# Adding three biases on TensorE instead of GpSimd in a stack of retention, experts and attention

## The reference, cut to what matters

```python
# x is (4, 512, 128): 4 sequences of 512 tokens, 128 channels
x = x + stack(layernorm(x))          # two layers of retention and feed-forward, below
x = x + experts(layernorm(x))        # the 2 best of 8 experts per token
x = x + attention(layernorm(x))      # causal, 16 heads of 8
x = x + experts(layernorm(x))

def stack(x):
    D = make_decay(512)
    for i in range(2):
        ln_x = layer_norm(x, ln1_g[i], ln1_b[i])
        q, k, v, xo = split(ln_x @ proj_w[i] + proj_b[i], 4)
        scores = einsum('bhld,bhmd->bhlm', q, k) * D
        ret = einsum('bhlm,bhmd->bhld', scores, v)        # 16 heads of 8, back to 128 channels
        ret = (ret * silu(xo)) @ reto_w[i] + reto_b[i]
        x = x + ret
        h = layer_norm(x, ln2_g[i], ln2_b[i])
        x = x + gelu(h @ ffn1_w[i] + ffn1_b[i]) @ ffn2_w[i] + ffn2_b[i]
    return layer_norm(x, lnf_g, lnf_b)

def attention(x):
    ...                                                   # q, k, v, causal softmax
    return out @ Wo.T + bo
```

## Time and profile before

| | |
|---|---|
| time, median of three runs (lowest to highest) | 947.39 us (946.0 to 948.69) |
| the profiled execution's own time | 948.85 us |
| its span in the profile | 947.0 us |
| mean granted clock of TensorE, share of full speed | 0.856 |
| instructions | 19447 |

### The profile page before, as it was taken

The page is one execution under the profiler, slowest core; times in us unless marked ns, Lnnn a source line. Parts: engine busy times, 40 slices in busy tenths (PEclk is TensorE's granted clock), DMA queues, the critical chain, the costliest instruction groups (busy, mean ns, idle before and its releaser), DMA issues. The chain is left out here.

```text
span 947.0 us, 19447 instructions
## 1 busy us (share of the span) xinstructions
PE 654.9 (69%) x6492; PEld 449.2 (47%) x6492; DVE 582.2 (61%) x1765; ACT 344.0 (36%) x597; POOL 356.8 (38%) x674
## 2 busy tenths in 40 slices
PE   2688784587885311999914589888778972499990
PEld 0345453244554311999912134444434441398990
DVE  7978833688925580666751477667458734366663
ACT  2223242333352411444405035545444561243430
POOL 1323321124352374677746300111311323367771
PEclk9799998799997555999966579989889995699995
DMA  9201299211120011555534710420420000254544
GB/s 227 83 23 46 83 185 165 67 45 49 43 62 1 17 51 49 158 156 152 158 110 111 161 24 3 104 46 8 119 48 9 19 18 12 76 164 129 164 136 142
DMA packets 100035, 81.02 MB, mean 86 GB/s; under 512 B 7516, under 2 KB 91932, under 8 KB 99196
## 3 DMA queue, kind: packets, MB, share of 16 engines
q1 hardware_dynamic: 95152, 70.18, 30.8%
q0 software_dynamic: 4544, 9.38, 2.9%
q10 hardware_dynamic: 240, 0.20, 0.1%
HBM read 54.56 MB, written 23.20 MB: 82 GB/s over the span
## 5 line engine op out<-in xcount | busy, mean ns | idle before, releaser
L1264 DVE TENSOR_REDUCE rmax<-PA 128x1 f32<-128x512 f32 (+3 forms) x256 | 120.4, 489 | 88.0 <-PE PA L1978 81.3
L756 POOL DMA_INDIRECT outs_dram<-va,ids x78 | 96.4, 1236 | 56.7 <-DVE va L1204 30.9
L741 POOL DMA_INDIRECT rows_dram<-va,idx x64 | 63.8, 997 | 104.5 <-DVE va L1147 86.7
L1935 PE MATMUL PC<-ffn_w,pm 128*128 128x128 f32 x624 | 88.3, 285 | 11.1 <-DMA ffn_w<-in_w 10.7
L1705 PE MATMUL P<-const,xn 128*128 128x128 f32 x92 | 18.7, 340 | 98.0 <-ACT xn L1487 32.8
L1978 PE MATMUL PA<-kst,qst 96*128 96x512 bf16 (+3 forms) x256 | 84.6, 336 | 0.0
L1935 PEld LDWEIGHTS PC<-ffn_w,pm 128*128 128x128 f32 x624 | 76.3, 193 | 14.7 <-DMA ffn_w<-in_w 13.9
L1194 DVE SCALAR_TENSOR_TENSOR pm<-PB,invb,decay 128x512 f32<-128x512 f32 x78 | 58.1, 745 | 38.0 <-ACT decay L1552 36.9
L1976 PE MATMUL PA<-mqb,idb 128*128 128x128 bf16 x256 | 60.7, 238 | 28.7 <-DMA qst<-qst 14.7
L1544 ACT ACTIVATE kv_b<-P 128x256 f16<-128x256 f16 x78 | 29.9, 383 | 132.4 <-PE P L1914 132.4
L1976 PEld LDWEIGHTS PA<-mqb,idb 128*128 128x128 bf16 x256 | 25.6, 100 | 90.2 <-issue 40.8
(11 more groups left out here) (241 smaller groups left out, 1491.8 us busy)
## 6 DMA issues: line engine op xcount, KB each, us to landing
ffn_w<-in_w SPq DMA_DIRECT2D x78, 256.0 KB, 2.9
rows_dram<-wall SPq DMA_DIRECT2D x1, 8385.0 KB, 50.7
X<-in_w SPq DMA_DIRECT2D x32, 256.0 KB, 2.9
proj_w<-rows_dram SPq DMA_DIRECT2D x78, 65.0 KB
qst<-parts_dram SPq DMA_DIRECT2D x12, 384.0 KB
kst<-parts_dram SPq DMA_DIRECT2D x12, 384.0 KB
parts_dram<-qkp SPq DMA_DIRECT2D x16, 256.0 KB, 2.6
X<-in_x SPq DMA_DIRECT2D x8, 256.0 KB, 4.5
```

Source lines behind the costliest of these rows:

```text
L741: nc.gpsimd.indirect_dma_start(out=rows_dram, out_offset=bass.IndirectOffsetOnAxis(ap=idx[:, t, r:r + 1], axis=0), in_=xrow[:, t, :], in_o ...
L756: nc.gpsimd.indirect_dma_start(out=outs_dram, out_offset=bass.IndirectOffsetOnAxis(ap=ids[:, k % YB:k % YB + 1], axis=0), in_=ysb[:, k % Y ...
L1264: nc.vector.tensor_reduce(rmax[:, i, h % HG:h % HG + 1], PA[:, n % 2, 0:(i + 1) * P], AX_X, ALU.max).then_inc(pair_sb[n % 2], 1)
L1935: ins = mm(PC[:, k % 2, 0:D], eT[:, k % 2, f, :], w2b[k % WB2][:, f, :], start=f == 0, stop=f == FB - 1)
```

## The change

The 20 additions of GpSimd go, with `add_bias` and its three callers, their three semaphores and VectorE's waits for these. In their place TensorE adds each bias to the accumulator: behind the matmul (or the four matmuls) that makes a tile's 128x128 result stands one more into the same place, with `start=False`, so that it accumulates. Its weights are `one_row`, a row of 128 ones on one partition (a part of the constants that are there already), and its moving operand is the bias's own row on partition 0: the product of a column of ones and a row. That is 32 float32 matmuls in retention (a tile and layer each), 32 in feed-forward and 16 in attention, 80 in all. The last matmul of a group now carries the count to the semaphore. The loads of the biases stay as they are.

```diff
--- before.py
+++ after.py
@@ -435,9 +435,6 @@
         state_sb = sem("state_sb")
         ro_ps = sem("ro_ps")
         ro_up = sem("ro_up")
-        reto_added = sem("reto_added")
-        ffn2_added = sem("ffn2_added")
-        bo_added = sem("bo_added")
         f1_ps = sem("f1_ps")
         f1_sb = sem("f1_sb")
         f2_ps = sem("f2_ps")
@@ -680,27 +677,6 @@
                 link(nc.gpsimd.tensor_tensor(w, y, mvr[:, b % 2, :, 0], ALU.mult))
                 nc.gpsimd.tensor_scalar(w, w, -1.0, None, ALU.mult).then_inc(nrm_sb, 1)
 
-            def add_bias(acc, s, bias):
-
-                r = slice(TPS * s, TPS * s + TPS)
-                return nc.gpsimd.tensor_tensor(acc[:, r, :], acc[:, r, :], bias.unsqueeze(1).to_broadcast([P, TPS, D]),
-                                               ALU.add)
-
-            def add_reto(layer, s):
-
-                pool.wait_ge(xn_ready, BY_DVE.index(1 + 2 * layer) * SEQ + s + 1)
-                add_bias(R, s, reto_b[:, layer, :]).then_inc(reto_added, 1)
-
-            def add_ffn2(layer, s):
-
-                pool.wait_ge(xn_act, BY_ACT.index(2 + 2 * layer) * SEQ + s + 1)
-                add_bias(R, s, ffn2_b[:, layer, :]).then_inc(ffn2_added, 1)
-
-            def add_bo(s):
-
-                pool.wait_ge(xn_act, BY_ACT.index(LNC) * SEQ + s + 1)
-                add_bias(X, s, bo[:, :]).then_inc(bo_added, 1)
-
             def decay_k(g):
 
                 pool.wait_ge(kv_sb, g + 1)
@@ -763,18 +739,9 @@
                     decay_k(layer * NT + t)
                     if t == 0 and layer == 0:
                         pool.wait_ge(in_ffn, in_ffn_n)
-                        for s in range(SEQ):
-                            add_reto(layer, s)
                     if t % TPS == 2 and t > TPS:
                         norm_factors(layer * SEQ + t // TPS - 1)
-                    if t % TPS == 1 and t > 2 * TPS:
-                        add_ffn2(layer, t // TPS - 2)
                 norm_factors(layer * SEQ + SEQ - 1)
-                for s in range(SEQ - 2, SEQ):
-                    add_ffn2(layer, s)
-                if layer + 1 < LAYERS:
-                    for s in range(SEQ):
-                        add_reto(layer + 1, s)
             pool.wait_ge(in_ffn, in_ffn_n)
             pool.wait_ge(rg_sb, LAYERS * NT)
             pool.wait_ge(re_ps, LAYERS * NT)
@@ -803,8 +770,6 @@
                     norm_factors(A + 2)
                     part_rests(1)
                     norm_factors(A + 3)
-                    for s in range(SEQ):
-                        add_bo(s)
                     for s in range(SEQ - 1):
                         if s + 2 < SEQ:
                             part_rests(s + 2)
@@ -949,7 +914,6 @@
                 def add_out(t):
                     g = layer * NT + t
                     dve.wait_ge(ro_ps, g + 1)
-                    dve.wait_ge(reto_added, g // TPS + 1)
                     nc.vector.tensor_tensor(R[:, t, :], PC[:, 0, 2 * D:3 * D], R[:, t, :], ALU.add).then_inc(ro_up, 1)
 
                 def sums(t):
@@ -1000,7 +964,6 @@
                     b = layer * SEQ + s
                     r = slice(TPS * s, TPS * s + TPS)
                     dve.wait_ge(f2_ps, b + 1)
-                    dve.wait_ge(ffn2_added, b + 1)
                     nc.vector.tensor_tensor(R[:, r, :], PC[:, b % 2, :].rearrange("p (k n) -> p k n", k=TPS),
                                             R[:, r, :], ALU.add).then_inc(f2_up, 1)
                     dve.wait_ge(f2_up, b + 1)
@@ -1296,7 +1259,6 @@
                 def add_out(s):
                     n = PAIR[("wo", s)]
                     dve.wait_ge(pair_ps, n + 1)
-                    dve.wait_ge(bo_added, s + 1)
                     r = slice(TPS * s, TPS * s + TPS)
                     nc.vector.tensor_tensor(X[:, r, :], PA[:, n % 2, :].rearrange("p (i n) -> p i n", i=TPS),
                                             X[:, r, :], ALU.add).then_inc(pair_sb[n % 2], 1)
@@ -1680,6 +1642,7 @@
         @block.tensor
         def _(pe):
             mm = nc.tensor.matmul
+            one_row = const[0:1, C_ONES:C_ONES + P]
 
             def ring(*key):
 
@@ -1829,7 +1792,8 @@
                     if g >= 1:
                         pe.wait_ge(ro_up, g)
                     o = PC[:, 0, 2 * D:3 * D]
-                    mm(o, rgT[:, g % 2, :], reto_w[:, layer, :], start=True, stop=True).then_inc(ro_ps, 1)
+                    mm(o, rgT[:, g % 2, :], reto_w[:, layer, :], start=True, stop=False)
+                    mm(o, one_row, reto_b[0:1, layer, :], start=False, stop=True).then_inc(ro_ps, 1)
 
                 def ahead_turn(s):
 
@@ -1883,8 +1847,9 @@
                                 count(0, 0).then_inc(ring_ps, 1)
                         bank = PC[:, b % 2, k * D:(k + 1) * D]
                         for f in range(FB):
-                            ins = mm(bank, hT[:, b % 2, f, k * P:(k + 1) * P], ffn2_w[:, layer, f, :], start=f == 0,
-                                     stop=f == FB - 1)
+                            mm(bank, hT[:, b % 2, f, k * P:(k + 1) * P], ffn2_w[:, layer, f, :], start=f == 0,
+                               stop=False)
+                        ins = mm(bank, one_row, ffn2_b[0:1, layer, :], start=False, stop=True)
                     ins.then_inc(f2_ps, 1)
 
 
@@ -2040,7 +2005,8 @@
                     wait_pair(pe, "ao", s)
                     for i in range(TPS):
                         o = bank[:, i * D:(i + 1) * D]
-                        ins = mm(o, aoT[:, i * P:(i + 1) * P], wo, start=True, stop=True)
+                        mm(o, aoT[:, i * P:(i + 1) * P], wo, start=True, stop=False)
+                        ins = mm(o, one_row, bo[0:1, :], start=False, stop=True)
                     ins.then_inc(pair_ps, 1)
 
                 def run(uses):
```

## The result

The changed kernel takes 971.58 us (median of four runs, 970.03 to 973.22) against 946.69 us for the kernel before beside it (944.77 to 948.69): a ratio of 1.0263, 95% interval 1.0234 to 1.0291, or 24.9 us slower. Forecast were 965.7 us, 18.3 us of loss, with a range of 953 to 973. The sign, the range and the main mechanism held; about a quarter of the loss was not in the sum, and the measured time lies nearer to the rival "dearer" (973.6 us) than to the forecast. The profiled execution took 973.22 us, 24.4 more than the profiled one of before.

A forecast was written before the change was run, and what follows sets the result against it. No engine fills the span; retention is bound by TensorE and VectorE, late feed-forward and routing by a dependent chain. Exposed biases, 6.8 + 5.7 + 2.3 + 3.5 = 18.3 us, gave 965.7 us, range 953 to 973.

The forecast's parts named there:

- dearer: Retention's cover too short: another nine biases pass (5.6 us) and one covered attention projection (2.3 us): 973.6 us; chance 0.15.
- The price of a bias, 0.62 us: TensorE, each bias between two 128x128 matmuls: 0.22 us for its columns plus two changes of shape at 0.2 us.
- The choice between the ends: Per bias on TensorE: 0.62 us if one row is treated like 32 rows (taken), 0.22 if like 96.
- cheap: All added matmuls on TensorE: one row runs like 96, no change of shape, 7.3 us lost, 954.7 us; chance 0.18.
- GpSimd worth nothing: Removing GpSimd's 20 additions, 25.5 us together, was credited with nothing; bounds 0 and 1 us gained.
- Feed-forward of layer 0, nothing: 16 biases there cost nothing, covered by VectorE's 13.74 us wait for the weights' largest values; without cover 10 us.
- Feed-forward of layer 1: Of 16 biases, 8 pass before the turn of sequence 3 (5.0 us), the last some 0.7: together 5.7 us.
- on an ordinary tile it is covered: Retention: TensorE's wait for VectorE hides the bias except where sequences end; 5.5 biases, 3.4 us per layer, 6.8 for both.
- the fourth projection: Attention output, last sequence: runs at half clock and everything waits for it; between 4 x 0.62 and 4 x 1.24, taken 3.5 us.
- the third: Attention output, third sequence's projection: no covering wait, so its four biases cost 3 x 0.62 + 0.42 = 2.3 us.
- The first two are covered: Attention output, projections of sequences 0 and 1: transfer waits of 2.62 and 4.55 us cover their 2.3 us of biases.
- a rival by which it could rise: Added matmuls keep TensorE's full clock in feed-forward, routing and last projection, 8.8 us faster: 945.9 or 956.9 us; chance 0.04.

The follow-up runs named there:

- 64-row kernel: The changed kernel with each bias 64 rows deep (ones times the bias in row 0, zeros below): 964.29 us, +18.6; again 966.72 us, +20.0 over the kernel before.
- the parts tested alone: The kernel before with one of the change's three edits each: retention 955.3 us (+10.6), feed-forward 952.52 us (+9.4), attention 953.41 us (+7.7).
- the change taken again: The changed kernel itself measured once more, nothing altered: 966.82 us against 942.2 us for the kernel before, +24.9 us.
- the change beside the 64-row kernel: The changed kernel measured once more, on one chip with the variant whose biases are 64 rows deep: 971.02 us, +25.9 us over the kernel before.
- Retention alone: The kernel before with only retention's bias moved to TensorE, 32 one-row matmuls: 955.3 us against 945.15 us, +10.6 us.

## Why the prediction was right, and where it was off

**The price of a bias, 0.62 us, was right**, and so was its split: 0.61 measured in feed-forward and behind a projection of retention, and 0.21 and 0.23 where the shape stays. The choice between the ends (one row like 32 rows, not like 96) decided the forecast; the other end was the rival "cheap", 7.3 us, and the kernels whose biases are 128 rows deep measured about that, +6.2 and +9.3. The sum of 18.3 us is what the 64-row kernel lost (+18.6 and +20.0), which pays for the changes of shape and for no lower clock. That it agrees so closely is partly luck: the parts tested alone cost 10.6, 9.4 and 7.7 us, where the sum has 6.8, 5.7 and 5.8.

**GpSimd worth nothing: right** (-0.1 us). Its decay of tile 1 now ends early (41.97 + 0.45 = 42.42 instead of 44.92), and the matmul that the earlier trace rows shows at 45.86 starts at 47.81, later than before.

**Feed-forward of layer 0, nothing: right, with little to spare.** The store's time in the queue shrank from 15.39 to 7.59 us and the wait from 13.74 to 3.07; behind retention's delay the store's issue slipped by another 7.8 us, where 5.0 were forecast, and a stretch at half clock stands there (124.1 to 130.9) that the kernel before has not. The wait's end moved by 7.5 us, as the filling of the table starts 8.0 later (115.17 before, behind retention's last maximum): only retention's delay passed.

```profile
123.15 0.43 SPq L575 DMA_DIRECT2D rows_dram<-wall  x1
...
160.89 7.59 SPq L568 DMA_DIRECT2D amax_dram<-amax  x1
...
177.13 1.98 DVE L838 TENSOR_REDUCE amax<-X 128x8 f32<-128x1024 f32 x1 [3.07 <-DMA X<-amax_dram]
```

In the profile of the change taken again this wait was zero: the cover had just run out. (The load had come early there, as the time from the start of the filling to the end of the store was 40.7 us instead of 45.3.)

**Feed-forward of layer 1: right.** The turn of sequence 3 starts at 295.41 instead of 280.98, 4.4 us later against the end of retention where 5.0 were forecast, and the whole stretch gives 5.2 against 5.7. The first row is the turn, the second the end of the last group's wait, 10.63 against 9.91 in the earlier trace rows:

```profile
295.41 0.66 PE L1668 MATMUL P<-const,xn 128*128 128x128 f32 x4
...
332.75 0.69 DVE L967 TENSOR_TENSOR R<-PC,R 128x512 f32<-128x512 f32 x1 [10.63 <-PE PC L1852]
```

**Retention: the step that failed is "on an ordinary tile it is covered".** It took the wait of 0.45 us as cover for a bias of 0.62. I had looked at which tiles have a wait, not at the sum of the waits. Who waited for whom on TensorE, from 45 to 118 us of the kernel before (line, releaser: us in total, times, longest):

```profile
PE PA L1794 <- DVE pm L915: 3.0, 7, 0.7
...
PE PC L1832 <- DVE vs L927: 1.4, 2, 1.0
PE PC L1812 <- DVE state L944: 1.3, 1, 1.3
PE P L1716 <- ACT xT L1390: 0.6, 1, 0.6
```

After the change, from 46 to 127 us, the first and the last are gone altogether and the other two have shrunk:

```profile
PE PC L1775 <- DVE state L909: 0.9, 1, 0.9
PE PC L1795 <- DVE vs L892: 0.8, 2, 0.4
```

So all the cover that layer 0 had was 3.0 + 0.6 + 0.6 + 0.4 = 4.6 us, for 13 biases of 0.62 and 3 of 0.42 (those ahead of matmuls of 32 columns), 9.3 us in all: 4.7 pass, not 3.4. This is the mechanism of the rival "dearer". The change beside the 64-row kernel bears the 4.7 out. From retention's first tiles to the filling of the table, its granted clock was as in the kernel before, and the filling started 4.9 us later (115.17 before); in the first profile of the change the clock was lower, and it started 8.0 later. The rows are windows of the kernel before, of the change, and of the change beside the 64-row kernel, and that one's filling:

```profile
46.00:115.00 69.00, 57.90 (x679) 34.25 (x677) 59.69 (x127) 18.28 (x31) 22.90 (x77) 0.98 0.13 40
...
46.00:123.00 77.00, 69.66 (x718) 41.46 (x718) 61.99 (x130) 18.27 (x31) 21.34 (x76) 0.93 0.10 36
...
46.00:120.00 74.00, 65.65 (x710) 39.07 (x708) 60.36 (x127) 18.28 (x31) 20.57 (x76) 0.98 0.12 37
...
120.08 0.43 SPq L575 DMA_DIRECT2D rows_dram<-wall  x1
```

The other 2.2 of layer 0's 6.9 us thus go with the lower clock of that one execution; that the one-row matmuls caused it is not shown, as kernels without them have such stretches too. Layer 1 lost only 2.5, so that both layers come to 9.4 us in the profile. Retention alone measured +10.6 us where 6.8 were forecast.

**Attention: the fourth projection was right, the third until the clock fell.** The first two are covered to within 1.1 us, by which the difference grows from the stage's start to the third. The fourth now runs at half clock with its biases between the blocks, and VectorE waits 7.42 us for it instead of 3.78, 3.6 us more where I took 3.5:

```profile
804.34 0.79 PE L2009 MATMUL PA<-bo,const 1*128 1x128 f32 x2
...
806.62 0.69 DVE L1263 TENSOR_TENSOR X<-PA,X 128x512 f32<-128x512 f32 x1 [7.42 <-PE PA L2009]
```

The third was priced at 2.3 and is 2.6 at its addition (it starts at 763.70 instead of 746.65, and 14.5 us of that were there already); the clock that fell within it added 3 us to the scores behind in the profiled execution. The sum held the clock constant, and named a rival by which it could rise, but none by which it falls. The 4 to 6 us between 64 rows and one, which go with a lower mean clock, are most of what the forecast lacks.

## What to carry to other kernels

An addition on an engine with slack costs nothing until a trace shows somebody waiting for it; moved to the engine that others wait for, even 80 tiny matmuls cost 25 us here. A matmul of few rows is priced by its neighbours' shapes: open an accumulation with it behind matmuls of the same depth, or make it as deep as its neighbours, before counting columns (here 8, and 6 to 9 us, instead of 25). Cover is a budget: add up the waits of a stage and compare the sum with what is added, instead of crossing off each place that has a wait.

## What the runs showed of the hardware

A 64-row matmul between 128-row ones costs the same two changes as a one-row one (0.41 us from the bias to its successor in both). Biases of 128 rows raised the mean granted clock to 0.866 where the kernel before had 0.860, and those of one row did not (0.858 and 0.855 beside 0.860), though all were dealt out in the same places; I had expected no difference. A one-row matmul behind 32-row ones cost 0.20 us, between 128-row ones 0.61.
